# Attention beside a dense layer: where a short piece of beside-work stands between the scores and values of two steps

## The chip, the cores and the metric

The kernel runs on one core of a Trainium2 chip. The metric is device time in microseconds, from one launch to its end, as the median of several runs. Engines are named as the profile names them: PE is TensorE (PEld its weight loads), ACT is ScalarE, DVE is VectorE, POOL is GpSimd, SP the engine that issues transfers.

## What is computed

A block of a transformer on x of shape 2 x 2048 x 1024: attention with small latents, then a dense layer with eight LoRA updates folded in, both with a residual.

```python
def attention(x, ...):           # 32 heads, latents: q 12, k and v 4
    C_q = x @ Wq_d + bq_d
    C_kv = x @ Wkv_d + bkv_d
    q = (C_q @ W_qk + b_qk).reshape(b, s, 32, 4)
    scores = einsum('bqhd,bkd->bhqk', q, C_kv) / sqrt(4)
    attn = softmax(scores, axis=-1)
    V = (C_kv @ Wv_u + bv_u).reshape(b, s, 32, 32)
    out = einsum('bhqk,bkhd->bqhd', attn, V)
    return out.reshape(b, s, 1024) @ Wo + bo

x = x + attention(layernorm(x), ...)
x = x + layernorm(x) @ W.T + bias + lora(layernorm(x))
```

## The kernel before

**Stages.** The kernel has a first stage (statistics, latents and queries, up to 105.8 us in the trace), an attention stage (105.8 to 2017 us) and a tail for the last 512 rows (to 2077.6 us). The change lies in the attention stage only.

**Chunks and steps.** The 4096 rows are eight chunks of 512 queries. A chunk has 128 steps (`STEPS`): eight groups of four heads, and for each group 16 tiles of 128 keys. A step has three parts:

- `scores(step)` (L892 to L905): four products of 27 rows each on PE, one for each head, written to 4 of the 6 PSUM banks that hold scores (`SCORE_SLOTS` = 3 slots of two banks). It waits until the exponentials of an earlier step have read the banks that it overwrites: the wait is `exp_done` of the first exponential of the step before.
- two exponentials on ACT (L634), each 128 x 1024, from PSUM to `probs`, a ring of three steps. The first one of a step also waits until `values` of three steps before has read its slot of the ring.
- `values(step)` (L907 to L915): four products with 32 columns each on PE (two passes each in the trace, so 8 matmul records a step), from `probs` into the PSUM bank `SUMS`. They run two to three steps behind the scores.

**What runs beside.** PE works off, between those, the pieces of other work that `beside` names. One piece belongs to each odd step. For chunks 1 to 7 (`dense_beside`) they are the back half of the chunk before: turning the sums (`turn_o`, `turn_back`), the output projection (`project`, three products), turning the normed rows (`turn_y`, eight pieces a chunk of four transpositions each, L943), and the dense layer (`dense_burst`, 44 pieces a chunk of 4 or 5 products of 512 columns, L959). All of these write one PSUM bank, `SHARED`, and DVE empties it between them. For chunk 0 (`prepare`) they are the preparation of the dense weights. Its main part are sixteen pairs: `turn_w(k)` (four transpositions of the weights, L868) and, one pair of steps later, `lora_update(k)` (one product of 512 columns, two passes in the trace, L873). After each of the two DVE runs its part of `move_w(k)` (L1374 to L1383): a copy behind the transpositions, and behind the product an addition (L1381), a rounding copy (L1184) and a subtraction (L1186), both of the last two into `w_eff`. `turn_w(k)` waits in `free_bank` for the semaphore `prep_ok`, which the last of these, for k - 1, raises.

**What sets the order.** It is written out by hand in `attention`. PE runs its instructions in the order of the code and stands at each wait. In an even step `s` and the odd one behind it the order is: scores(s), values(s-2), values(s-1), scores(s+1), the piece beside step s+1. The other engines have programs of their own and are tied to PE by semaphores alone.

Of the kernel before, what the change touches and what calls it, by code (L numbers as in the profile page):

```python
# [33 lines left out]
def build_block(nc, x, wq_d, bq_d, w_qk, b_qk, wkv_d, bkv_d, wv_u, bv_u, wo, bo,  # L34
# [14 lines left out]
    CHUNKS = T // N  # L49
    CB = S // N  # L50
    TT = N // P
    KT = S // P
    KB = D // P
    G4 = H // 4
# [18 lines left out]
    with ExitStack() as ctx:  # L73
# [113 lines left out]
        prep_ok = sem("prep_ok")  # L187
# [29 lines left out]
        bound_read = sem("bound_read")  # L217
# [18 lines left out]
        q_loaded = [sem("q_loaded0"), sem("q_loaded1")]  # L236
# [3 lines left out]
        o_moved = sem("o_moved")  # L240
# [7 lines left out]
        ffn_moved = sem("ffn_moved")  # L248
# [19 lines left out]
        STEPS = G4 * KT  # L268
        BEHIND = 2
        UNITS = 2 * TT  # L270

        START = 2
# [3 lines left out]
        Q_LOADS = 16 * 4  # L276
# [5 lines left out]
        SCORE_SLOTS = 3  # L282
        SUMS, SHARED = 6, 7
# [5 lines left out]
        TURN_BACK_AT = BEHIND + 3  # L289
        FIRST_AT = BEHIND + 5  # L290
        TILE_AT, NEXT_AT, DENSE_AT = [], [], []
        at = FIRST_AT + 4
        for t in range(TT):
            if t == 2:
                TURN_AT = at
# [6 lines left out]
            at = low[-1] + 2  # L302
# [356 lines left out]
        def _(pe):  # L659
# [113 lines left out]
            def keep_busy(times, bank):  # L773
                for _ in range(times):
                    nc.tensor.transpose(ps[:, bank, 0:P], wqk_sb[:, :], ident[:, :])  # L775
# [100 lines left out]
            def prepare(g, kt):  # L876
                step = g * KT + kt
                if step == VALUES_AT:
                    turn_values()
                if step in (VALUES_AT + 2, VALUES_AT + 4):  # L880
                    turn_lora(PREP_LORA + (step - VALUES_AT) // 4)
                if WO_AT <= step < WO_AT + 16 and step % 2:
                    i = (step - WO_AT) // 2
                    times_wo(PREP_VO + i // 2, lv if i < 4 else bv_wide, i % 2)
                if step in (BIAS_AT, BIAS_AT + 2):
                    sum_bias(PREP_BIAS + (step - BIAS_AT) // 2)
                for k in range(2 * KB):
                    at = W_AT + 4 * k if k < W_BEFORE else TURN_0_AT + 2 + 4 * (k - W_BEFORE)
                    if step == at:
                        turn_w(k)  # L890
                    if step == at + 2:
                        lora_update(k)  # L892


            def scores(c, b, step, first):

                g, kt = divmod(step, KT)
                i = 2 * (c * STEPS + step)
                if step or not first:
                    pe.wait_ge(exp_done, i - 1)  # L900
                for h in range(4):
                    at = 2 * ((i + h // 2) % SCORE_SLOTS) + h % 2
                    last = nc.tensor.matmul(ps[:, at, :], key_t[TILE * h:TILE * h + KEYS, bass.ts(b * KT + kt, P)],  # L903
                                            q_in[TILE * h:TILE * h + KEYS, g % 2, :], start=True, stop=True)
                    if h % 2:  # L905
                        last.then_inc(s_ready, 1)

            def values(c, b, step):

                g, kt = divmod(step, KT)  # L910
                at = CW - W5 * (g % 4)
                pe.wait_ge(exp_done, 2 * (c * STEPS + step) + 2)
                for h in range(4):
                    last = nc.tensor.matmul(ps[32 * h:32 * h + 32, SUMS, :], c_wide[:, b * KT + kt, at:at + 32],  # L914
                                            probs[:, (c * STEPS + step) % PROBS, bass.ts(h, N)], start=(kt == 0 and g % 4 == 0),  # L915
                                            stop=(kt == KT - 1 and g % 4 == 3))
                last.then_inc(pv_done, 1)

            def turn_o(c, half):

                pe.wait_ge(o_moved, 2 * c + half + 1)
                for t in range(TT):
                    last = nc.tensor.transpose(ps[:, SHARED, bass.ts(t, P)], o_sb[:, bass.ts(t, P)], ident[:, :])
                last.then_inc(o_turned, 1)
# [39 lines left out]
            def dense_beside(c, step):  # L964

                p = c - 1
                if step == TURN_BACK_AT:
                    turn_back(p)
                if step == FIRST_AT:
                    pe.wait_ge(o_t_ready, p + 1)  # L970
                    project(p, 0, 0, SHARED)
                if step == FIRST_AT + 2:
                    pe.wait_ge(y_ready, START + p * TT * 2 + 1)
                    project(p, 0, 1, SHARED)
                if step == TURN_AT:
                    pe.wait_ge(ffn_moved, START + (p * TT + 2) * 2)
                    turn_o(c, 0)
                for t in range(TT):
                    if step == TILE_AT[t]:
                        if t == 2:  # L980
                            pe.wait_ge(o_normed, 2 * c + 1)
                        elif t:
                            pe.wait_ge(ffn_moved, START + (p * TT + t) * 2)
                        pe.wait_ge(y_ready, START + (p * TT + t + 1) * 2)
                        turn_y(p, t, 0, SHARED)
                    if step == TILE_AT[t] + 2:
                        pe.wait_ge(t_moved, START + CHUNKS * KB + (p * TT + t) * 2 + 1)
                        turn_y(p, t, 1, SHARED)
                    if t < TT - 1 and step == NEXT_AT[t]:
                        pe.wait_ge(ffn_moved, START + (p * TT + t) * 2 + 1)  # L990
                        project(p, t + 1, 0, SHARED)
                    if t < TT - 1 and step == NEXT_AT[t] + 2:
                        pe.wait_ge(y_ready, START + (p * TT + t + 1) * 2 + 1)
                        project(p, t + 1, 1, SHARED)
                    for half in range(2):
                        if step in DENSE_AT[t][half]:
                            j = DENSE_AT[t][half].index(step)
                            if j == 0 and half == 0:
                                pe.wait_ge(t_moved, START + CHUNKS * KB + (p * TT + t + 1) * 2)
                            elif j == 0 and t < TT - 1:  # L1000
                                pe.wait_ge(y_ready, START + (p * TT + t + 2) * 2)
                            elif j == 0:
                                pe.wait_ge(ffn_moved, START + (p * TT + t) * 2 + 1)
                            dense_burst(p, t, half, j)

            def attention(c, b, b_before=None):
                first = b_before is None
                for g in range(G4):
                    for kt in range(KT):
                        step = g * KT + kt  # L1010
                        scores(c, b, step, first)
                        if first and step < BEHIND:
                            keep_busy(8, SHARED if step else 2 * SCORE_SLOTS - 1)
                        if kt == KT - 1 and c * G4 + g + 1 < CHUNKS * G4:
                            pe.wait_ge(q_loaded[(g + 1) % 2], ((c * G4 + g + 1) // 2 + 1) * Q_LOADS)
                        if step % 2 == 0:
                            if step == 0 and not first:
                                values(c - 1, b_before, STEPS - 2)
                                values(c - 1, b_before, STEPS - 1)
                            if step:  # L1020
                                if first and step == BEHIND:
                                    pe.wait_ge(bound_read, 2)
                                if (step - BEHIND) % (4 * KT) == 0 and not (first and g == 0):
                                    pe.wait_ge(o_moved, 2 * c + g // 4)
                                values(c, b, step - 2)
                                values(c, b, step - 1)
                        if kt == BEHIND + 1 and g == 0 and not first:

                            pe.wait_ge(ffn_moved, START + (c - 1) * TT * 2)
                            turn_o(c - 1, 1)  # L1030
                        if first and step == TURN_0_AT:
                            pe.wait_ge(prep_ok, PREP_W + 2 * W_BEFORE)
                            turn_o(c, 0)
                        if first:
                            prepare(g, kt)
                        else:
                            dense_beside(c, step)

            pe.wait_ge(q_loaded[0], Q_LOADS)
            attention(0, 0)  # L1040
# [513 lines left out]
```

## Time and profile before

| | us |
|---|---|
| median of 3 runs | 2078.73 |
| lowest and highest run | 2078.69, 2080.83 |
| the profiled execution | 2079.62 |
| its span, first to last instruction | 2077.6 |
| up to the first exponential | 105.8 |
| chunk 0 of the attention (first exponential to that of chunk 1) | 237.50 |
| each of chunks 2 to 6 | 239.07 to 239.09 |
| from the last exponential's start | 61.6 |

PE is busy 94% of the span, ACT 95%, DVE 23%, POOL 10%. The busy time of an engine is the union of its instructions; exponentials overlap by about a tenth of a microsecond, so a late start of less than that does not show as idle time, and the start times have to be read. In what follows a pair of steps is called by the piece beside it, and the length of a pair is the time from one pair's first scores to the next one's.

### The profile page before, as it was taken

To read this page: it belongs to the slowest core of one execution; us is meant where nothing else is said; L and a number is where in the kernel's file an instruction comes from. 1 tells how busy PE (TensorE), PEld (TensorE's weight loads), DVE (VectorE), ACT (ScalarE), POOL (GpSimd) and SP (SyncE) were. 2 spreads that over 40 slices of the span, in tenths; PEclk is the share of its full clock that TensorE was granted. 3 is DMA by queue.
4 is the path that set the end of the run, shared out by engine and by line. 5 is a ranking of instruction groups with operands and counts; after the bars stand their busy time and mean duration, and the time that the engine had idled before them with its cause. 6 is when DMAs were issued, how large, how long until landed. Compare 5 with 4: busy or idle time off the path is not lost.

```text
span 2077.6 us, 36033 instructions
## 1 busy us (share of the span) xinstructions
PE 1962.2 (94%) x15085; PEld 715.1 (34%) x15085; DVE 475.6 (23%) x1140; ACT 1969.5 (95%) x2185; POOL 214.9 (10%) x220
## 2 busy tenths in 40 slices
PE   7979898999999999999999999999999999999999
PEld 4522222333333333333333333333333333333337
DVE  7713333111121211211121111212111111212115
ACT  5799999999999999999999999999999999999980
POOL 5600000000110002000110001100110001100022
PEclk9999999999999999999999999999999999999999
DMA  8442000000010001000010000100010000100011
GB/s 308 147 137 86 3 26 26 5 25 13 26 35 15 13 26 46 5 13 26 26 35 3 26 25 13 36 15 26 13 46 5 26 13 26 35 15 13 26 41 41
DMA packets 45806, 77.42 MB, mean 37 GB/s; under 512 B 15886, under 2 KB 29766, under 8 KB 45642
## 3 DMA queue, kind: packets, MB, share of 16 engines
q1 hardware_dynamic: 43296, 75.02, 10.7%
q8 instruction: 119, 1.95, 0.4%
q10 hardware_dynamic: 2346, 0.09, 0.1%
q14 instruction: 45, 0.37, 0.1%
HBM read 51.23 MB, written 23.86 MB: 36 GB/s over the span
## 4 chain that ended last, share of the span: by engine, by line
ACT 43%; PE 35%; issue 16%; DVE 0%; DVEq 0%
ACT probs L634 43%; PE ps L914 17%; PE ps L959 10%; PE ps L903 6%; PE ps L948 2%; PE ps L937 0%; PE ps L943 0%; PE ps L775 0%; DVE y L1433 0%; PE ps L1056 0%; PE ps L1052 0%; DVE o_t L1489 0%; ACT o_t L649 0%; ACT o_sb L646 0%; DVE recip L1481 0%
## 5 line engine op out<-in xcount | busy, mean ns | idle before, releaser
L634 ACT ACTIVATE probs<-ps 128x1024 f32<-128x1024 f32 x2048 | 1899.8, 1030 | 17.7 <-PE ps L903 7.1
L914 PE MATMUL ps<-probs,c_wide 128*32 128x512 f32 x8192 | 985.7, 599 | 0.0
L903 PE MATMUL ps<-q_in,key_t 27*128 27x512 bf16 x4096 | 404.2, 385 | 94.1 <-ACT probs L634 90.8
L959 PE MATMUL ps<-w_eff,xn_t 128*128 128x512 f32 x1344 | 394.5, 418 | 0.0
L914 PEld LDWEIGHTS ps<-probs,c_wide 128*32 128x32 f32 x8192 | 212.3, 108 | 424.9 <-issue 220.0
L903 PEld LDWEIGHTS ps<-q_in,key_t 27*128 27x128 bf16 x4096 | 103.0, 91 | 722.7 <-ACT probs L634 715.2
L1433 DVE SCALAR_TENSOR_TENSOR y<-ps,nw,y 128x512 f32<-128x512 f32 x64 | 48.1, 751 | 979.0 <-PE ps L959 967.6
L959 PEld LDWEIGHTS ps<-w_eff,xn_t 128*128 128x128 f32 x1344 | 228.2, 188 | 102.1 <-issue 69.8
L536 POOL TENSOR_TENSOR y<-y,ffn_bias 128x1024 f32<-128x1024 f32 x32 | 76.4, 2388 | 1349.9 <-DVEq L1454 1349.9
L531 POOL TENSOR_TENSOR y<-y,attn_bias 128x1024 f32<-128x1024 f32 x32 | 75.9, 2385 | 463.9 <-DMA y<-in_L_attn_x_dram 463.8
L1417 DVE TENSOR_TENSOR y<-ps,y 128x512 f32<-128x512 f32 x56 | 38.7, 692 | 134.9 <-PE ps L937 134.9
L1184 DVE CAST xn_t<-ps 128x512 fp32r<-128x512 f32 x56 | 38.8, 692 | 123.3 <-PE ps L943 123.3
L937 PE MATMUL ps<-w_vo,o_t 128*128 128x512 f32 x192 | 60.4, 426 | 0.3 <-DVE o_t L1489 0.3
L556 ACT ACTIVATE area<-ps 128x512 f32<-128x512 f32 x64 | 35.3, 616 | 26.4 <-PE ps L678 22.0
L948 PE MATMUL ps<-w_eff,xn_t 128*128 128x512 f32 x192 | 44.7, 391 | 0.0
L943 PE MATMUL ps<-ident,y 128*128 128x128 f32 x256 | 41.0, 285 | 0.1
L1186 DVE TENSOR_TENSOR xn_t<-ps,xn_t 128x512 fp32r<-128x512 f32 x56 | 38.8, 692 | 9.8 <-DVEq L1120 9.8
L1420 DVE BATCH_NORM_STATS2 stats<-y 128x6 f32<-128x512 f32 x56 | 38.9, 695 | 1.9
L948 PEld LDWEIGHTS ps<-w_eff,xn_t 128*128 128x128 f32 x192 | 35.8, 188 | 7.3
L937 PEld LDWEIGHTS ps<-w_vo,o_t 128*128 128x128 f32 x192 | 31.4, 188 | 16.4 <-issue 12.7
L654 ACT ACTIVATE xn_t<-ps 128x512 fp32r<-128x512 f32 x8 | 4.4, 596 | 34.1 <-PE ps L943 34.1
L943 PEld LDWEIGHTS ps<-ident,y 128*128 128x128 f32 x256 | 27.1, 140 | 13.7 <-issue 13.3
(168 smaller groups left out, 619.7 us busy)
## 6 DMA issues: line engine op xcount, KB each, us to landing
y<-in_L_attn_x_dram SPq DMA_DIRECT2D x40, 512.0 KB, 4.3
out_dram<-y SPq DMA_DIRECT2D x31, 512.0 KB, 2.7
area<-in_L_attn_x_dram SPq DMA_DIRECT2D x16, 512.0 KB, 9.1
q_in<-q_parts SPq DMA_DIRECT2D x256, 27.0 KB
q_parts<-q_parts_sb SPq DMA_DIRECT2D x48, 128.0 KB, 2.8
xn<-in_L_attn_x_dram SPq DMA_DIRECT2D x8, 512.0 KB, 7.7
y<-in_L_attn_Wo_dram SPq DMA_DIRECT2D x1, 2048.0 KB, 8.6
xn<-in_L_attn_Wo_dram SPq DMA_DIRECT2D x1, 2048.0 KB, 13.3
```

What stands on the lines that cost most here:

```text
L531: pool.tensor_tensor(y[:, t, :], y[:, t, :], attn_bias[:, :], ALU.add).then_inc(xb_ready, 1)
L536: pool.tensor_tensor(y[:, t, :], y[:, t, :], ffn_bias[:, :], ALU.add).then_inc(yb_ready, 1)
L634: nc.scalar.activation(probs[:, (c * STEPS + step) % PROBS, bass.ts(pair, 2 * N)], ps[:, 2 * (i % SCORE_SLOTS):2 * (i % SCORE_SLOTS) + 2, ...
L903: last = nc.tensor.matmul(ps[:, at, :], key_t[TILE * h:TILE * h + KEYS, bass.ts(b * KT + kt, P)], q_in[TILE * h:TILE * h + KEYS, g % 2, :] ...
L914: last = nc.tensor.matmul(ps[32 * h:32 * h + 32, SUMS, :], c_wide[:, b * KT + kt, at:at + 32], probs[:, (c * STEPS + step) % PROBS, bass.t ...
L937: last = nc.tensor.matmul(ps[:, bank, :], o_t[:, a, bass.ts(t, P)], w_vo[:, b, bass.ts(n, N)], start=(i == 0), stop=(i == 2))
L943: last = nc.tensor.transpose(ps[:, bank, bass.ts(a, P)], y[:, t, bass.ts(4 * u + a, P)], ident[:, :])
L948: last = nc.tensor.matmul(ps[:, bank, :], xn_t[:, t % 2, a, kb, :], w_eff[:, b, kb, bass.ts(half, N)], start=(kb + i == 0), stop=(kb == KB ...
L959: last = nc.tensor.matmul(ps[:, SHARED, :], xn_t[:, t % 2, a, kb, :], w_eff[:, b, kb, bass.ts(half, N)], start=(kb + i == 0), stop=(kb == ...
L1184: ch.then(nc.vector.tensor_copy(high, bank_part))
L1420: ch.put(nc.vector.bn_stats(stats[:, t, n, :], y[:, t, bass.ts(n, N)]))
L1433: nc.vector.scalar_tensor_tensor(out=y[:, t, bass.ts(half, N)], in0=ps[:, bank, :], scalar=nw[:, 0, 3, t:t + 1], in1=y[:, t, bass.ts(half, ...
```

## The change

In the pairs whose piece is a set of transpositions, and in pairs of chunk 0 that have no piece left, the piece and the scores of the second step go between the two sets of values. All other pairs keep their order. The loop body is split into two helpers, `score` (the scores with their waits) and `beside` (the piece with its waits).

```diff
+            TURN_STEPS = [BEHIND + 1, TURN_BACK_AT, TURN_AT] + [at + 2 * u for at in TILE_AT for u in range(2)]
+            PREP_TURN_STEPS = [W_AT + 4 * k if k < W_BEFORE else TURN_0_AT + 2 + 4 * (k - W_BEFORE) for k in range(2 * KB)]
+            PREP_LAST = PREP_TURN_STEPS[-1] + 2
...
+                for step in range(0, STEPS, 2):
+                    score(step)
+                    if first:
+                        between = step and (step + 1 in PREP_TURN_STEPS or step + 1 > PREP_LAST)
+                    else:
+                        between = step + 1 in TURN_STEPS
+                    if step:
...
+                        values(c, b, step - 2)
+                    elif not first:
+                        values(c - 1, b_before, STEPS - 2)
+                        values(c - 1, b_before, STEPS - 1)
+                    if between:
+                        beside(step + 1)
+                        score(step + 1)
+                        values(c, b, step - 1)
+                    else:
+                        if step:
+                            values(c, b, step - 1)
+                        score(step + 1)
+                        beside(step + 1)
```

With the numbers of this kernel, `TURN_STEPS` are the odd steps 3, 5, 11, 13, 41, 43, 71, 73, 75, 103 and 105: eleven pairs in each of chunks 1 to 7, in five groups of neighbours (2, 2, 2, 3 and 2). `PREP_TURN_STEPS` are 53, 57, 69, 73 and so on by fours to 121: sixteen pairs of chunk 0, each with a `lora_update` pair behind it. Behind them steps 125 and 127 have no piece. Only PE's order changes; ACT, DVE, POOL and SP run the same instructions in the same order.

PE in chunk 0, around one `turn_w` (L868) between two `lora_update` (L873). `ps` is the PSUM, L903 are scores, L914 values (four products a step), `xn` holds the weights to be turned here. Before:

```order
L903 MATMUL ps<-q_in,key_t 128x512 x4
L873 MATMUL ps<-lora_bt,lora_a_sb 128x512
L903 MATMUL ps<-q_in,key_t 128x512 x4
L914 MATMUL ps<-probs,c_wide 32x512 x8
L903 MATMUL ps<-q_in,key_t 128x512 x4
L868 MATMUL ps<-ident,xn 128x128 x4
L903 MATMUL ps<-q_in,key_t 128x512 x4
L914 MATMUL ps<-probs,c_wide 32x512 x8
L903 MATMUL ps<-q_in,key_t 128x512 x4
L873 MATMUL ps<-lora_bt,lora_a_sb 128x512
```

And now:

```order
L903 MATMUL ps<-q_in,key_t 128x512 x4
L873 MATMUL ps<-lora_bt,lora_a_sb 128x512
L903 MATMUL ps<-q_in,key_t 128x512 x4
L914 MATMUL ps<-probs,c_wide 32x512 x4
L868 MATMUL ps<-ident,xn 128x128 x4
L903 MATMUL ps<-q_in,key_t 128x512 x4
L914 MATMUL ps<-probs,c_wide 32x512 x4
L903 MATMUL ps<-q_in,key_t 128x512 x4
L914 MATMUL ps<-probs,c_wide 32x512 x8
L903 MATMUL ps<-q_in,key_t 128x512 x4
L873 MATMUL ps<-lora_bt,lora_a_sb 128x512
```

The transpositions stand one set of values and one set of scores nearer to the product before them.

PE in a chunk from 1 on, at two neighbouring `turn_y` pairs (L943, which turns rows of `y`) behind a projection (L937). Before:

```order
L937 MATMUL ps<-w_vo,o_t 128x512 x3
L903 MATMUL ps<-q_in,key_t 128x512 x4
L914 MATMUL ps<-probs,c_wide 32x512 x8
L903 MATMUL ps<-q_in,key_t 128x512 x4
L943 MATMUL ps<-ident,y 128x128 x4
L903 MATMUL ps<-q_in,key_t 128x512 x4
L914 MATMUL ps<-probs,c_wide 32x512 x8
L903 MATMUL ps<-q_in,key_t 128x512 x4
L943 MATMUL ps<-ident,y 128x128 x4
```

And now:

```order
L937 MATMUL ps<-w_vo,o_t 128x512 x3
L903 MATMUL ps<-q_in,key_t 128x512 x4
L914 MATMUL ps<-probs,c_wide 32x512 x4
L943 MATMUL ps<-ident,y 128x128 x4
L903 MATMUL ps<-q_in,key_t 128x512 x4
L914 MATMUL ps<-probs,c_wide 32x512 x4
L903 MATMUL ps<-q_in,key_t 128x512 x4
L914 MATMUL ps<-probs,c_wide 32x512 x4
L943 MATMUL ps<-ident,y 128x128 x4
L903 MATMUL ps<-q_in,key_t 128x512 x4
L914 MATMUL ps<-probs,c_wide 32x512 x4
```

The second scores of such a pair no longer stand behind the values of step s-1.

## Rows read from the trace of the kernel before

**Rows 1.** The page's costliest group: line, operation, count | busy us, mean ns | idle.

```profile
L634 ACT ACTIVATE probs<-ps 128x1024 f32<-128x1024 f32 x2048 | 1899.8, 1030 | 17.7 <-PE ps L903 7.1
```

**Rows 2.** Table by stretch, chunks 0 and 3: length, busy time by engine, clock.

```profile
core 0: us, PE busy (x) PEld busy (x) DVE busy (x) ACT busy (x) POOL busy (x), PEclk, DMA share, GB/s
105.78:343.28 237.50, 205.47 (x1725) 56.63 (x1728) 72.40 (x123) 236.56 (x257) 9.50 (x4) 0.99 0.19 60
821.50:1060.57 239.07, 230.38 (x1800) 80.50 (x1796) 41.34 (x107) 237.57 (x257) 18.95 (x8) 1.00 0.07 22
```

**Rows 3.** Timeline of PE, one pair of chunk 1: start us, length, what.

```profile
502.76 0.40 PE L903 MATMUL ps<-q_in,key_t 27*128 27x512 bf16 x4
503.08 1.92 PE L914 MATMUL ps<-probs,c_wide 128*32 128x512 f32 x16
504.94 0.39 PE L903 MATMUL ps<-q_in,key_t 27*128 27x512 bf16 x4
505.27 1.20 PE L959 MATMUL ps<-w_eff,xn_t 128*128 128x512 f32 x4
506.45 0.40 PE L903 MATMUL ps<-q_in,key_t 27*128 27x512 bf16 x4
```

**Rows 4.** Timeline of ACT there, single exponentials (507.19 left out).

```profile
504.40 1.04 ACT L634 ACTIVATE probs<-ps 128x1024 f32<-128x1024 f32 x1
505.37 1.03 ACT L634 ACTIVATE probs<-ps 128x1024 f32<-128x1024 f32 x1
506.29 1.02 ACT L634 ACTIVATE probs<-ps 128x1024 f32<-128x1024 f32 x1
...
508.10 1.04 ACT L634 ACTIVATE probs<-ps 128x1024 f32<-128x1024 f32 x1
```

**Rows 5.** Timeline of ACT, neighbouring exponentials at the attention's start.

```profile
106.70 1.02 ACT L634 ACTIVATE probs<-ps 128x1024 f32<-128x1024 f32 x1
107.60 1.03 ACT L634 ACTIVATE probs<-ps 128x1024 f32<-128x1024 f32 x1
```

**Rows 6.** Chain of waits, pairs with five products beside: start, us, what.

```profile
518.10 1.85 PE ps L914 x16
519.95 0.33 PE ps L903 x4
520.28 1.36 PE ps L959 x5
521.63 0.33 PE ps L903 x4
```

**Rows 7.** Timeline of chunk 0, one cycle from `lora_update` to `lora_update`.

```profile
297.07 1.12 PE L873 MATMUL ps<-lora_bt,lora_a_sb 128*128 128x512 f32 x2
298.25 0.40 PE L903 MATMUL ps<-q_in,key_t 27*128 27x512 bf16 x4
...
299.78 0.69 DVE L1186 TENSOR_TENSOR w_eff<-part_f,w_eff 128x512 fp32r<-128x512 f32 x1 [0.18 <-DVEq L1120]
300.44 0.40 PE L903 MATMUL ps<-q_in,key_t 27*128 27x512 bf16 x4
300.76 0.66 PE L868 MATMUL ps<-ident,xn 128*128 128x128 f32 x4
...
304.45 1.13 PE L873 MATMUL ps<-lora_bt,lora_a_sb 128*128 128x512 f32 x2
```

**Rows 8.** Timeline of chunk 0, the one `turn_w` that waited for DVE.

```profile
322.40 0.69 DVE L1186 TENSOR_TENSOR w_eff<-part_f,w_eff 128x512 fp32r<-128x512 f32 x1 [0.18 <-DVEq L1120]
323.15 0.66 PE L868 MATMUL ps<-ident,xn 128*128 128x128 f32 x4 [0.18 <-DVE w_eff L1186]
```

**Rows 9.** Timeline of PE, first stage, transpositions with work right behind them.

```profile
50.17 0.66 PE L678 MATMUL ps<-ident,area 128*128 128x128 f32 x4
50.67 0.60 PE L722 MATMUL ps<-ident,lat 128*128 128x128 f32 x4
```

**Rows 10.** Timeline of chunk 3, the first `turn_y` pair behind a dense half.

```profile
895.41 0.75 DVE L1433 SCALAR_TENSOR_TENSOR y<-ps,nw,y 128x512 f32<-128x512 f32 x1 [18.04 <-PE ps L959]
897.79 0.66 PE L943 MATMUL ps<-ident,y 128*128 128x128 f32 x4
898.97 0.39 PE L903 MATMUL ps<-q_in,key_t 27*128 27x512 bf16 x4 [0.53 <-ACT probs L634]
```

**Rows 11.** Table by stretch, 3.4 us at the attention's start.

```profile
107.30:110.70 3.40, 3.40 (x20) 1.83 (x24) 1.55 (x3) 3.34 (x5) 0.00 (x0) 0.51 0.63 63
```

More of the change, by code:

```diff
@@ L1004, in dense_beside @@
                             dense_burst(p, t, half, j)
+            TURN_STEPS = [BEHIND + 1, TURN_BACK_AT, TURN_AT] + [at + 2 * u for at in TILE_AT for u in range(2)]
+            PREP_TURN_STEPS = [W_AT + 4 * k if k < W_BEFORE else TURN_0_AT + 2 + 4 * (k - W_BEFORE) for k in range(2 * KB)]
+            PREP_LAST = PREP_TURN_STEPS[-1] + 2
             def attention(c, b, b_before=None):
                 first = b_before is None
[L1008 to L1037, printed above, removed]
@@ new lines, in score, with beside @@
+                def score(step):
+                    scores(c, b, step, first)
+                    g, kt = divmod(step, KT)
+                    if first and step < BEHIND:
+                        keep_busy(8, SHARED if step else 2 * SCORE_SLOTS - 1)
+                    if kt == KT - 1 and c * G4 + g + 1 < CHUNKS * G4:
+                        pe.wait_ge(q_loaded[(g + 1) % 2], ((c * G4 + g + 1) // 2 + 1) * Q_LOADS)
+                def beside(step):
+                    if step == BEHIND + 1 and not first:
+                        pe.wait_ge(ffn_moved, START + (c - 1) * TT * 2)
+                        turn_o(c - 1, 1)
+                    if first and step == TURN_0_AT:
+                        pe.wait_ge(prep_ok, PREP_W + 2 * W_BEFORE)
+                        turn_o(c, 0)
+                    if first:
+                        prepare(*divmod(step, KT))
+                    else:
+                        dense_beside(c, step)
@@ new lines, in attention @@
+                for step in range(0, STEPS, 2):
+                    score(step)
+                    if first:
+                        between = step and (step + 1 in PREP_TURN_STEPS or step + 1 > PREP_LAST)
+                    else:
+                        between = step + 1 in TURN_STEPS
+                    if step:
+                        if first and step == BEHIND:
+                            pe.wait_ge(bound_read, 2)
+                        if (step - BEHIND) % (4 * KT) == 0 and not (first and step == BEHIND):
+                            pe.wait_ge(o_moved, 2 * c + step // (4 * KT))
+                        values(c, b, step - 2)
[6 more added lines that the diff above has]
+                        values(c, b, step - 1)
+                    else:
+                        if step:
+                            values(c, b, step - 1)
+                        score(step + 1)
+                        beside(step + 1)
```

## The prediction, made before the changed kernel was run

> **What bounds the kernel now.** I began with the page's costliest groups: 2048 exponentials on ACT, 1899.8 us busy and 17.7 us idle [rows 1]. The table by stretch says the same of each chunk: ACT is busy 236.56 of 237.50 us in chunk 0 and 237.57 of 239.07 in chunk 3, beside a PE that is busy 205 and 230 us [rows 2]. That looks like a full ACT, and the start times show that it is not quite one. Two exponentials that wait for nothing start 0.90 us apart (106.70, 107.60) [rows 5], and from 506.29 to 508.10 there are two such distances, 0.905 each [rows 4]. So four exponentials, a pair of steps, could take 3.61 us. The pair in the timeline takes 3.69: from scores at 502.76 to scores at 506.45 [rows 3].
>
> The timelines show what the 0.08 us are. The distances between exponentials are 0.97 (504.40 to 505.37), 0.92 (to 506.29), 0.90 and 0.90 [rows 4]. The late one is the first exponential of the second step, and it is late by PE's order: its scores stand behind both sets of values. Read as a ring it is: exponential, 1.03 long, and 0.05 until PE starts the first scores; 0.32 until the values; 1.86 for both sets of values (503.08 to 504.94); 0.43 until the exponential of the second scores (504.94 to 505.37) [rows 3, 4]. The sum, 1.08 + 0.32 + 1.86 + 0.43 = 3.69, is the length of the pair. The piece beside is not in that ring as long as it ends before 1.08 + 0.43 = 1.51 us after the second scores began. With five products it does not: 0.33 + 1.85 + 0.33 + 1.36 = 3.87 us, and PE alone sets the pair [rows 6]. The change does not touch those pairs. So each pair is bound by one of three: ACT at 3.61, the ring at 3.69, PE at 3.87.
>
> **The pairs of chunks 1 to 7.** In a moved pair the second scores come behind one set of values and the transpositions. I price these: half of 1.86 is 0.93, and I allow 1.00, since leaving 32-column products costs once more. For four transpositions the rows bound the time until something else can start: 0.50 (50.17 to 50.67, other transpositions behind) [rows 9] and 0.66, their whole busy time [rows 10]. I take 0.58, between the two, as scores are products of another shape but the busy time overlaps what follows by 0.07, as in 0.40 against 0.32 for scores [rows 3]. The way from the first exponential to that of the next moved scores is then 1.08 + 0.32 + 1.00 + 0.58 + 0.43 = 3.41 us (3.49 with 0.66), under ACT's 3.61. The other conditions hold too: scores(s+1) need the first exponential of step s, 1.51 us against a distance of 1.81; values(s-1) end 1.3 us after scores(s+1) start, while scores(s+2) may start after 1.51 and the slot of the ring of three is wanted later. So ACT sets a moved pair.
>
> The transpositions start 1.18 us earlier in the pair than now. In the tightest place, a tile's first `turn_y`, DVE's addition ends at 895.41 + 0.75 = 896.16 and the transpositions now start at 897.79, so that 896.61 is still 0.45 late enough [rows 10]. The other turns read what DVE finished a pair before, or stand behind a turn that has itself moved; I cost them at nothing. If the cover were gone, PE would stand and the 3.41 would grow, up to 0.2 us of it free.
>
> The gain: an exponential behind a late one comes at 0.92, so the first moved pair of a group gives 3.69 - (0.92 + 3 x 0.903) = 0.06 us, a later one 3.69 - 3.61 = 0.08. The pair behind a group is back in the ring at 3.69. A chunk has five groups with eleven pairs: 5 x 0.061 + 6 x 0.078 = 0.77 us, and seven chunks **gain 5.4 us**. Bounds: nothing, if ACT has a slower floor than the two rows show; and no more than this, as ACT can't go below it.
>
> **The pairs of chunk 0.** Here the moved transpositions have a wait that is now covered. `turn_w(k)` needs the whole of `move_w(k-1)` on DVE, which starts behind `lora_update(k-1)`. In the rows the product starts at 297.07 and DVE's subtraction ends at 299.78 + 0.69 = 300.47, 3.40 later. Now the transpositions stand behind the second scores of the next pair, at 300.76, so that DVE is just done [rows 7]. In the new order they could go at 298.25 + 0.32 + 1.00 = 299.57 and have to stand until 300.47 plus the way from DVE to PE. That way is 0.06 us: once in this trace `turn_w` did wait, and started at 323.15 behind an end at 323.09 [rows 8]. PE stands 0.96 us at the wait, and behind it in its queue are scores(s+1), the values and the scores of the next pair; ACT waits for the first of those. No other engine is late by it.
>
> The cycle from one `lora_update` to the next, step by step: 3.40 to the end on DVE, 0.06 to PE, 0.58 for the transpositions, 0.43 from the scores to the exponential, 1.08 from the exponential to the first scores of the unmoved pair behind, 0.33, 1.86 for both sets of values, 0.32 for the second scores. Sum 8.06 us, against 304.45 - 297.07 = 7.38 now [rows 7]: 0.68 more. It happens for k = 1 and for k = 3 to 15, 14 times: 9.5 us. `turn_w(0)` and `turn_w(2)` have no `lora_update` in the pair before them, so these two gain 0.06 each, and the two pairs without a piece at the end gain 0.06 + 0.08. The chunk's boundary may give back 0.1. Chunk 0 **loses 9.2 to 9.3 us**. Bounds of the stall term: with 0.50 for the transpositions 14 x 0.60 = 8.4, with 0.66 14 x 0.76 = 10.6.
>
> **Sum.** 9.2 - 5.4 = +3.8 us, on the profiled execution 2079.62 + 3.8 = 2083.4. That execution was 0.9 above the median of the runs, so the median goes from 2078.73 to **2082.5 us**, 0.18% more. The bounds of the terms give 2081.4 to 2083.6. A measurement here can tell about 0.2% (4.2 us, 2082.9) from no change, so my likeliest case ends just inside that.
>
> **Rivals.**
>
> *The stall is covered, and the kernel gets faster.* If DVE's `move_w` were done by the time PE arrives at the moved transpositions, all sixteen `turn_w` pairs would gain 0.06 and chunk 0 would give 16 x 0.06 + 0.14 + 0.1 = 1.2 us on top of 5.4: 2072.1 us. It decides at 299.57 against 300.53 in the rows; DVE would have to be a full microsecond quicker from the product's start, with three dependent operations in between. For it speaks only that DVE has nothing else to do there. 5%.
>
> *ACT does not close up.* If the moved pairs stay at 3.69 for a reason of ACT's own, only the loss is left: 2078.73 + 9.5 = 2088.2 us. For it: no pair of this trace runs at 3.61 from end to end. Against it: two distances of 0.90 in a row behind a late one [rows 4] and one of two first steps [rows 5]. The Trainium skill (ScalarE: Activation LUTs, What ACT_TABLE_LOAD costs) gives 186 ns plus 0.833 ns an element for an ACTIVATE with immediates and an overlap of 93 ns, for 1024 elements an estimate of 0.95 us from start to start; by that rule four take 3.78 and nothing at all could be gained. The pair of 3.69 is already below it. 7%.
>
> *PE's clock falls in chunk 0.* At the start of the attention, where PE had stood idle and then did transpositions only, the granted clock was 0.51, the lower of the levels 1.2 and 2.4 GHz, for 3.4 us [rows 11]. If the new stalls brought that on, each fall would cost at most 1.7 us (3.4 us at half speed do 1.7 us of work), from 2084.2 for one to 2106 for one in each of the 14 cycles. Against it: PE stays busy for some 6.8 of the 8.06 us of the stalled cycle (four scores at 0.32, two times 1.86, 0.58 and 1.12), and the clock is 1.00 in the chunks [rows 2]. The Trainium skill (TensorE: Matmul & The Clock Gate, Part 4: PE-mode transpose) says that transpositions do not count as PE activity in the way of products; by that rule the moved stretch, stall and transpositions together, is the likeliest place for a fall. 4%.
>
> *It is as reckoned*, with the loss of chunk 0 larger than the gain of the others. 84%.
>
> **How the numbers follow.** The likeliest case is 2082.5, with 2081.2 to 2083.9 as its own range. Leaving out 2 in 10, I take 2080.6 to 2084.6, which has room for a half-covered stall, for one fall of the clock and for the run-to-run spread of the runs shown (2078.69 to 2080.83). Slower by over 0.2%, above 2082.9: four tenths of the likeliest case, 0.33, with 0.07 and 0.03 of the rivals, 0.43. Faster: 0.05. Within: 0.52.
>
> **What would show it.** The table by stretch: chunk 0 near 246.8 us instead of 237.50, each of chunks 2 to 6 near 238.3 instead of 239.07. The waits: PE at L868 on DVE `w_eff` for 0.9 to 1.0 us, 14 times. Exponentials 0.90 apart through a moved pair of a later chunk. A chunk 0 of 236 us would make the stall wrong, later chunks of 239.1 the gain, and a clock under 0.98 in chunk 0 the assumption that it holds.

## The result

The changed kernel takes 2086.64 us (median of 8 runs, 2084.94 to 2088.84) against 2079.68 us for the kernel before (8 runs, 2078.69 to 2080.83). The ratio is 1.0034, with a 95% interval of 1.0025 to 1.0044: 7.0 us **slower**. The forecast was 3.8 us slower, 2082.5 us, with a range from 2080.6 to 2084.6 us. The profiled execution took 2088.10 us, its span is 2086.3 us.

Shown are the page's costliest group, then the table by stretch: chunk 0, chunk 1, chunk 3 and what follows the last exponential's start (columns: length, busy time by engine, clock, DMA).

```profile
L634 ACT ACTIVATE probs<-ps 128x1024 f32<-128x1024 f32 x2048 | 1898.9, 1041 | 26.2 <-PE ps L903 15.7
```

```profile
core 0: us, PE busy (x) PEld busy (x) DVE busy (x) ACT busy (x) POOL busy (x), PEclk, DMA share, GB/s
105.67:352.61 246.94, 208.84 (x1725) 54.93 (x1728) 72.07 (x123) 237.51 (x256) 9.48 (x4) 0.99 0.18 58
352.61:591.59 238.98, 232.06 (x1800) 79.38 (x1796) 41.21 (x106) 237.48 (x258) 14.26 (x6) 1.00 0.05 15
830.38:1069.18 238.80, 231.88 (x1800) 79.39 (x1796) 41.34 (x107) 237.31 (x258) 18.99 (x8) 1.00 0.07 22
2023.48:2086.30 62.82, 58.28 (x273) 46.17 (x272) 32.64 (x97) 7.20 (x18) 14.41 (x6) 0.97 0.17 59
```

Beside [rows 2]: chunk 0 went from 237.50 to 246.94, 9.4 us more and as forecast (246.8); 0.14 of it lie in the last but one of the stalls below, where DVE's rounding copy took 0.57 us in this execution and 0.43 elsewhere. Chunk 3 went from 239.07 to 238.80. It should have been 238.3, so a chunk gained 0.27 us and not 0.77. That is where the forecast fails. The tail is 1.2 us longer in this one execution, with a clock of 0.97; more on that below. In the group row the mean exponential is 1041 ns where it was 1030 [rows 1]: exponentials in the moved pairs are recorded as longer, and the rows of ACT below show how.

**The stall in chunk 0**, in the waits of PE alone and in the timeline of one cycle (start us, length, engine, what):

```profile
PE ps L868 <- DVE w_eff L1205: 12.5, 14, 1.0
```

```profile
303.02 1.12 PE L873 MATMUL ps<-lora_bt,lora_a_sb 128*128 128x512 f32 x2
304.20 0.40 PE L903 MATMUL ps<-q_in,key_t 27*128 27x512 bf16 x4
304.53 1.07 PE L914 MATMUL ps<-probs,c_wide 128*32 128x512 f32 x8
...
305.72 0.69 DVE L1205 TENSOR_TENSOR w_eff<-part_f,w_eff 128x512 fp32r<-128x512 f32 x1 [0.18 <-DVEq L1139]
306.47 0.66 PE L868 MATMUL ps<-ident,xn 128*128 128x128 f32 x4 [0.88 <-DVE w_eff L1205]
307.06 0.39 PE L903 MATMUL ps<-q_in,key_t 27*128 27x512 bf16 x4
```

It stands 14 times. From the product's start at 303.02 to DVE's end at 306.41 are 3.39 us (forecast 3.40), 0.06 to PE, 0.59 until the scores (forecast 0.58). Beside [rows 7] the transpositions no longer find DVE done.

**The moved pairs of a later chunk.** The timeline of ACT in chunk 3, single exponentials of the two `turn_y` pairs (steps 10 to 13) and the first late one behind them; several between them are left out:

```profile
848.79 1.03 ACT L634 ACTIVATE probs<-ps 128x1024 f32<-128x1024 f32 x1
850.60 1.05 ACT L634 ACTIVATE probs<-ps 128x1024 f32<-128x1024 f32 x1
852.41 1.08 ACT L634 ACTIVATE probs<-ps 128x1024 f32<-128x1024 f32 x1
854.21 1.10 ACT L634 ACTIVATE probs<-ps 128x1024 f32<-128x1024 f32 x1
856.93 1.14 ACT L634 ACTIVATE probs<-ps 128x1024 f32<-128x1024 f32 x1
857.99 1.03 ACT L634 ACTIVATE probs<-ps 128x1024 f32<-128x1024 f32 x1
```

The first and the fifth row lie nine exponentials apart: (856.93 - 848.79) / 9 = 0.904 us from start to start, as forecast. But the durations climb from 1.03 to 1.14, 12.5 ns with each exponential. The ends are 849.82 and 858.07, so **an exponential is finished every 0.917 us**, not every 0.904. PE waits for ends, as its scores show (timeline of PE, the pair behind the group):

```profile
855.37 0.39 PE L903 MATMUL ps<-q_in,key_t 27*128 27x512 bf16 x4 [0.37 <-ACT probs L634]
855.70 1.92 PE L914 MATMUL ps<-probs,c_wide 128*32 128x512 f32 x16
857.55 0.40 PE L903 MATMUL ps<-q_in,key_t 27*128 27x512 bf16 x4
```

The scores at 855.37 wait for the exponential that started at 854.21 and ended at 855.32, and from there the ring runs as ever: 0.32, 1.86 and 0.43 to the exponential at 857.99. It starts 1.06 us behind the one before instead of 0.97 [rows 4]. What the starts had won in the group is given back there, except for some 0.024 us a pair: 3.690 - 4 x 0.917 = 0.022, and by the chunks (239.07 - 238.80) / 11 = 0.025.

### The profile page after: what moved, and what is told of

Read it like the earlier page. It is cut to its first block, busy times and chain, and to the rows that moved or that the text cites. A ratio compares the mean times of both kernels' runs of the same rounds, so it can differ in the third digit from the quotient of the medians.

```text
span 2086.3 us, 36034 instructions
## 1 busy us (share of the span) xinstructions
PE 1977.5 (95%) x15085; PEld 706.9 (34%) x15085; DVE 475.3 (23%) x1140; ACT 1968.8 (94%) x2185; POOL 215.3 (10%) x220
## 4 chain that ended last, share of the span: by engine, by line
ACT 38%; PE 35%; issue 11%; DVE 0%; DVEq 0%
ACT probs L634 38%; PE ps L914 16%; PE ps L959 10%; PE ps L903 6%; PE ps L948 2%; PE ps L937 0%; PE ps L943 0%; PE ps L1075 0%; DVE y L1452 0%; DVE w_eff L1205 0%; PE ps L868 0%; PE ps L1071 0%; DVE o_t L1508 0%; ACT o_t L649 0%; ACT o_sb L646 0%
## 5 line engine op out<-in xcount | busy, mean ns | idle before, releaser
L634 ACT ACTIVATE probs<-ps 128x1024 f32<-128x1024 f32 x2048 | 1898.9, 1041 | 26.2 <-PE ps L903 15.7
L914 PE MATMUL ps<-probs,c_wide 128*32 128x512 f32 x8192 | 1005.3, 600 | 0.0
L903 PE MATMUL ps<-q_in,key_t 27*128 27x512 bf16 x4096 | 404.1, 385 | 75.4 <-ACT probs L634 70.3
L903 PEld LDWEIGHTS ps<-q_in,key_t 27*128 27x128 bf16 x4096 | 102.9, 91 | 705.8 <-ACT probs L634 697.8
L914 PEld LDWEIGHTS ps<-probs,c_wide 128*32 128x32 f32 x8192 | 202.9, 108 | 389.2 <-issue 224.7
L937 PE MATMUL ps<-w_vo,o_t 128*128 128x512 f32 x192 | 61.9, 435 | 0.3 <-DVE o_t L1508 0.3
L943 PEld LDWEIGHTS ps<-ident,y 128*128 128x128 f32 x256 | 27.2, 140 | 47.5 <-issue 29.3
L943 PE MATMUL ps<-ident,y 128*128 128x128 f32 x256 | 40.9, 285 | 0.0
L937 PEld LDWEIGHTS ps<-w_vo,o_t 128*128 128x128 f32 x192 | 32.4, 193 | 16.6 <-issue 12.7
```

Source lines behind the costliest of these rows:

```text
L634: nc.scalar.activation(probs[:, (c * STEPS + step) % PROBS, bass.ts(pair, 2 * N)], ps[:, 2 * (i % SCORE_SLOTS):2 * (i % SCORE_SLOTS) + 2, ...
L937: last = nc.tensor.matmul(ps[:, bank, :], o_t[:, a, bass.ts(t, P)], w_vo[:, b, bass.ts(n, N)], start=(i == 0), stop=(i == 2))
L943: last = nc.tensor.transpose(ps[:, bank, bass.ts(a, P)], y[:, t, bass.ts(4 * u + a, P)], ident[:, :])
```

## The experiments

All times are medians, each beside the median of the kernel before on the same chip; times of stretches are from the one trace of each version. A traced execution can lie some us off the median. "Theory of ends" is the reading above; "theory of starts" that of the prediction.

### Each half of the change alone

Chunk 0's `turn_w` pairs unmoved:

```diff
-                        between = step and (step + 1 in PREP_TURN_STEPS or step + 1 > PREP_LAST)
+                        between = step + 1 > PREP_LAST
```

> The changed kernel with the sixteen turn_w pairs of chunk 0 in their old order; the eleven pairs of each later chunk and the two pieceless pairs stay moved. Theory of ends: back to back, exponentials start 0.904 us apart but finish 0.917 apart, and the ring of the next unmoved pair starts from an end, so a moved pair gains 3.690 - 4 x 0.917 = 0.024 us and the 79 moved pairs 1.9 us in all; with the boundary of chunk 0, 2.0 us faster than before. Theory of starts (the one of the prediction): 5.6 us faster. Either way chunk 0 is back at 237.4 us and no turn_w waits for DVE. The chunks from 2 on: 238.80 us by ends, 238.30 by starts.

Measured: 2077.36 us against 2079.34, ratio 0.9991 (0.9982 to 1.0000), 2.0 us faster. Table by stretch, chunks 0 and 3:

```profile
105.71:343.72 238.01, 206.50 (x1725) 57.21 (x1729) 72.14 (x123) 236.51 (x256) 9.49 (x4) 0.99 0.19 60
821.48:1060.26 238.78, 231.88 (x1800) 79.41 (x1796) 41.34 (x107) 237.29 (x258) 18.95 (x8) 1.00 0.07 22
```

The gain is the 2.0 of the theory of ends, and the 5.6 of the theory of starts are outside the interval (up to 3.7). Chunk 3 is at 238.78 (238.80 by ends, 238.30 by starts). Chunk 0 is 0.6 longer than expected, because the clock was at half for 6.8 us around its start where it was for 3.4 in the first trace of the kernel before: its first two pairs take 9.11 us against 8.44 there.

Chunk 0's `turn_w` pairs alone:

```diff
-                        between = step and (step + 1 in PREP_TURN_STEPS or step + 1 > PREP_LAST)
+                        between = step and step + 1 in PREP_TURN_STEPS
                     else:
-                        between = step + 1 in TURN_STEPS
+                        between = False
```

> Only the sixteen turn_w pairs of chunk 0 are moved, everything else is in the old order. If the loss is the 14 stalls of PE behind DVE's subtraction, chunk 0 takes 246.9 us, 9.5 more, later chunks 239.07, and the whole is 9.5 us slower than before. A rival, by which part of the loss belongs to the later chunks or the tail, has chunk 0 longer by less and the whole slower by clearly under 9 us.

Measured: 2089.02 us against 2079.34, ratio 1.0046 (1.0032 to 1.0059), 9.7 us slower. Chunk 3 is at 239.05 us again, chunk 0 at 246.24:

```profile
106.22:352.46 246.24, 207.15 (x1725) 54.55 (x1728) 72.21 (x123) 237.56 (x256) 9.48 (x4) 1.00 0.19 58
830.69:1069.74 239.05, 230.34 (x1800) 80.47 (x1796) 41.34 (x107) 237.56 (x257) 18.98 (x8) 1.00 0.07 22
```

This execution had no half clock at the start, which makes chunk 0 shorter by 1.0 us (last experiment). Against that, its last stall but one was 0.28 us longer than the others, as DVE's rounding copy took 0.71 us there. With both set right chunk 0 is at 247.0, against the 246.9 expected. The rival, by which part of the loss lies in the later chunks or the tail, is out. The halves add up: 9.7 - 2.0 = 7.7, beside 7.0 measured for both.

### What the transpositions wait for

The change as it is, with DVE releasing the bank as soon as it has read it:

```diff
                 ch.then(nc.vector.tensor_tensor(base, ps[:, SHARED, :], base, ALU.add))
                 ch.end()
-                split_three_pass(w_eff[:, 0, kb, cols], w_eff[:, 1, kb, cols], base, prep_ok)
+                dve.sem_inc(prep_ok, 1)
+                split_three_pass(w_eff[:, 0, kb, cols], w_eff[:, 1, kb, cols], base, w_split)
...
             pe.wait_ge(prep_ok, PREP_ALL)
+            pe.wait_ge(w_split, 2 * KB)
```

> The changed kernel as it is, but DVE gives the shared bank free right behind the addition that reads it (L1381 of before) and not behind the two operations on w_eff that follow; those raise a semaphore of their own, which PE awaits before chunk 1. DVE's way from the product's start to the release falls from 3.40 to some 2.1 us, under the 2.5 us that PE takes to the transpositions. If that wait is the loss of chunk 0, it falls to 237.1 us and the whole is 2.4 us faster than before (6.5 by the theory of starts). If anything else about the place of the transpositions is the loss, chunk 0 stays near 247.

Measured: 2077.23 us against 2079.34, ratio 0.9990 (0.9981 to 0.9999), 2.1 us faster. Timeline of chunk 0 (line numbers are one higher on PE; L869 are the transpositions):

```profile
297.19 1.12 PE L874 MATMUL ps<-lora_bt,lora_a_sb 128*128 128x512 f32 x2
298.37 0.39 PE L904 MATMUL ps<-q_in,key_t 27*128 27x512 bf16 x4
298.42 0.69 DVE L1402 TENSOR_TENSOR part_f<-ps,part_f 128x512 f32<-128x512 f32 x1 [4.50 <-PE ps L874]
...
299.69 0.66 PE L869 MATMUL ps<-ident,xn 128*128 128x128 f32 x4
299.99 0.69 DVE L1207 TENSOR_TENSOR w_eff<-part_f,w_eff 128x512 fp32r<-128x512 f32 x1 [0.18 <-DVEq L1141]
```

The transpositions start 1.32 us behind the scores, where the forecast put them (1.32 for scores and one set of values), with no idle time of PE, and before DVE's subtraction begins. Chunk 0 takes 236.95 us where the change took 246.94. Both executions had 3.4 us of half clock at the start. So the loss of chunk 0 is the wait for all of `move_w`, and of that the part that only concerns `w_eff`. The rest is the theory of ends once more: 2.1 us gained where 2.4 were due by ends and 6.5 by starts.

### The piece behind the second values

The moved pairs in the order scores, values, scores, values, piece:

```diff
                     if between:
-                        beside(step + 1)
                         score(step + 1)
                         values(c, b, step - 1)
+                        beside(step + 1)
```

> The same pairs as in the change, in the order scores, values, scores, values, piece: the scores of the second step are freed from the second values, but the transpositions stay at the end of the pair. They then start 2.64 us into the pair (two scores at 0.32 and two values at 1.00), behind DVE's end at 2.22 into it, so the stall should be gone: chunk 0 at 237.1 us. By ends the whole is 2.4 us faster than before (95 moved pairs of 0.024 and the boundary), by starts 6.5 us faster. A rival, by which it is the freed scores themselves that cost chunk 0 its 9.5 us, leaves chunk 0 near 247.

Measured: 2082.14 us against 2079.34, ratio 1.0013 (1.0004 to 1.0022), 2.8 us slower. A miss of both theories. Table by stretch, chunks 0 and 3, and the timeline of PE at the end of the same two `turn_y` pairs:

```profile
104.85:342.00 237.15, 206.46 (x1725) 54.30 (x1728) 72.21 (x123) 237.12 (x256) 9.48 (x4) 1.00 0.20 60
820.52:1059.68 239.16, 231.86 (x1800) 79.38 (x1796) 41.33 (x107) 237.66 (x257) 18.98 (x8) 1.00 0.07 22
```

```profile
843.75 0.39 PE L903 MATMUL ps<-q_in,key_t 27*128 27x512 bf16 x4 [0.37 <-ACT probs L634]
844.07 1.06 PE L914 MATMUL ps<-probs,c_wide 128*32 128x512 f32 x8
845.07 0.66 PE L943 MATMUL ps<-ident,y 128*128 128x128 f32 x4
845.66 0.39 PE L903 MATMUL ps<-q_in,key_t 27*128 27x512 bf16 x4
845.98 1.92 PE L914 MATMUL ps<-probs,c_wide 128*32 128x512 f32 x16
```

The stall is gone here too: chunk 0 is at 237.15, not 247 (with the full clock at its start, worth 1.0), so it is not the freed scores that cost 9.5 us. But a chunk now takes 239.16, more than the 239.07 of the kernel before. The trace is of the fastest of the eleven runs (2078.91), with the clock full throughout; it is 0.5 us above the median (2078.4) of the eight runs of the kernel before that had the full clock too. The remaining 2.3 us of the 2.8 lie in executions with falls of the clock, of which this version has no trace. The scores that open the pair behind the group start at 845.66 with no wait for ACT before them: PE comes to them late, with values and transpositions (0.32 + 1.00 + 0.59 = 1.91 us) behind scores that had themselves waited for an exponential. ACT has a reserve against that inside the group; the ring behind it has none. That PE's lateness is the whole of the 0.37 us between this chunk and that of the change is worked out from these rows and not tested by itself. In chunk 0 the pairs alternate, each moved one has an unmoved one behind it, and the same cost falls due sixteen times: by the first exponentials of the pairs, a moved pair takes 3.61 us and the one behind it 3.82, together 0.05 more than two unmoved ones, where the version with the early release has 3.62 and 3.74, 0.03 less.

### ACT's floor, with nothing beside

The early release, and the pairs of chunk 0 without a piece moved as well:

```diff
+            IDLE_STEPS = [s for s in range(5, TURN_0_AT, 2) if s < VALUES_AT or BIAS_AT + 2 < s < W_AT or s > W_AT + 4 * W_BEFORE - 2]
...
-                        between = step and (step + 1 in PREP_TURN_STEPS or step + 1 > PREP_LAST)
+                        between = step and (step + 1 in PREP_TURN_STEPS or step + 1 > PREP_LAST or step + 1 in IDLE_STEPS)
```

> The early release of the bank with 14 pairs more of chunk 0 moved, those that have no piece beside them: steps 4 to 18 (eight pairs in a row, 32 exponentials), 46 to 50 and 60 to 64. It measures ACT's floor with nothing beside on PE. Theory of ends: in the row of eight the starts stay 0.904 apart, each exponential lasts 12.5 ns longer than the one before, to 1.03 + 32 x 0.0125 = 1.43 us, and the pair behind the row pays all of it, its second scores' exponential coming some 0.40 us later than in a pair of the ring, 1.36 instead of 0.96 behind the one before; or the starts fall to 0.917 apart once the two are too far from each other. Either way a moved pair gains 0.024 us, chunk 0 goes from 236.9 to 236.6 and the whole is 2.4 us faster than before. A rival, that it is the transpositions beside that lengthen the exponentials: then these pairs show durations that stay near 1.03, the row of eight gains 0.078 a pair, and chunk 0 falls to 235.9.

Measured: 2076.37 us against 2080.36, ratio 0.9984 (0.9975 to 0.9993), 4.0 us faster by the medians, 1.5 to 5.2 by the interval. The 2.4 expected lie within it, and the times do not tell this version from the one before; its trace does. Timeline of ACT in the row of eight pairs (single exponentials, those between left out) and the first one behind it, with one set of scores of PE in the same stretch:

```profile
116.49 1.09 ACT L635 ACTIVATE probs<-ps 128x1024 f32<-128x1024 f32 x1
123.72 1.19 ACT L635 ACTIVATE probs<-ps 128x1024 f32<-128x1024 f32 x1
131.86 1.30 ACT L635 ACTIVATE probs<-ps 128x1024 f32<-128x1024 f32 x1
135.49 1.35 ACT L635 ACTIVATE probs<-ps 128x1024 f32<-128x1024 f32 x1
136.41 1.34 ACT L635 ACTIVATE probs<-ps 128x1024 f32<-128x1024 f32 x1
136.89 0.39 PE L904 MATMUL ps<-q_in,key_t 27*128 27x512 bf16 x4 [0.44 <-ACT probs L635]
137.32 1.35 ACT L635 ACTIVATE probs<-ps 128x1024 f32<-128x1024 f32 x1
...
143.16 1.02 ACT L635 ACTIVATE probs<-ps 128x1024 f32<-128x1024 f32 x1
```

From 116.49 to 131.86 are 17 exponentials: starts 0.904 apart, ends (117.58 and 133.16) 0.917 apart. The duration climbs by 12.5 ns each, with no piece on PE, so transpositions have nothing to do with it, and the rival is out. PE's scores come early enough there: the exponential at 131.86 starts 0.47 us behind its scores, where one that waits for them starts 0.43 behind. So nothing but ACT holds the ends at 0.917, and that is ACT's floor for this instruction. It settles the question of the two theories.

At 1.35 us the climb stops, and the starts themselves fall to 0.91 to 0.92 apart (136.41, 137.32). What stops it is the ring between ACT and PE, and not a limit of ACT that these rows could show: the scores at 136.89 wait for the exponential that started at 135.49 and ended at 136.83, and the exponential of these scores starts at 137.32, 0.43 behind them. Two exponentials then take 1.35 + 0.06 + 0.43 = 1.83 us, 2 x 0.917, and the starts can run ahead no further. This is read from the rows and not tested by an edit; how long durations could grow with more banks for scores is open. The exponential behind the row is the one at 143.16, a late one with its 1.02 us; the pair in which it stands takes 4.01 us where its like take 3.69, which pays back what the starts had won.

Chunk 0 is at 235.37 us, 1.6 less than in the version before it. Of that 1.0 is the clock at its start, full in this execution; 0.34 are the 14 pairs; and the three pairs at steps 16, 48 and 64 had been 0.09 longer than their neighbours in every trace with the old order, which they are no longer. The reason of that is open. So what the theory of ends says of the 14 pairs is met; the rest by which chunk 0 lies under the 236.6 expected is the clock and these three pairs.

### The clock in the first pairs and in the tail

Four single executions, of the two kernels unchanged.

> The kernel before, unchanged, for a second trace. Its first trace has one stretch of 3.4 us with the granted clock at half, at the start of the attention. Theory of the clock: these stretches come and go between executions of the same program, at the start of the attention (1.0 us each, from the first pairs of steps there) and in the tail (1.5 us each), and the eight chunks in between keep their times to 0.1 us. Then the time is 2078.6, 2079.6 or 2081.1 us for none, the first, or both. A rival, that the spread lies in the chunks themselves, has chunks that differ between the traces by more than that.

> The kernel before once more, for a third trace, with the same expectations: 2078.6, 2079.6 or 2081.1 us by the falls of the clock, and chunks equal to 0.1 us.

> The changed kernel, unchanged, for a second trace. Its first trace has two stretches of half clock, one at the start of the attention and one in the tail, and took 2088.1 us, 1.5 more than the median of its runs. Theory of the clock: without the second it takes 2086.6 us, without both 2085.6, with chunk 0 at 246.9 (246.0 without the fall at its start) and the later ones at 238.80 in every trace. A rival, that the change lengthens the tail by itself, has the tail 1.2 us longer than that of the kernel before also with no fall in it.

> The changed kernel once more, for a third trace, with the same expectations: 2085.6, 2086.6 or 2088.1 us by the falls of the clock, and chunks from 2 on at 238.80 us.

Measured: 2079.16 and 2079.57 us for the kernel before, 2087.07 and 2086.30 for the changed one. Table by stretch: the changed kernel's second of these (chunk 0, chunk 3, tail), then 6.8 us at the start of the attention in the first one of the kernel before, then 3.4 us in the tail of the changed kernel's first trace:

```profile
106.27:352.09 245.82, 207.44 (x1725) 54.31 (x1728) 71.93 (x123) 237.41 (x257) 9.48 (x4) 1.00 0.19 58
830.10:1068.90 238.80, 231.89 (x1800) 79.43 (x1800) 41.34 (x106) 237.29 (x257) 18.99 (x8) 1.00 0.07 22
2022.88:2084.50 61.62, 57.02 (x273) 44.96 (x272) 32.62 (x97) 7.22 (x18) 14.42 (x6) 1.00 0.17 60
```

```profile
103.30:110.10 6.80, 5.96 (x32) 3.67 (x36) 2.31 (x5) 4.31 (x5) 0.00 (x0) 0.50 0.52 70
```

```profile
2028.80:2032.20 3.40, 3.40 (x11) 2.62 (x10) 1.41 (x6) 0.49 (x2) 2.38 (x1) 0.50 0.45 146
```

The granted clock at the start of the attention was full in this trace; it was at 0.50 for 3.4 us in the changed kernel's other two traces, and for 3.4, 6.8 and 3.4 us in those of the kernel before. Chunk 0 is 245.82 us with it full and 246.94 in the changed kernel's first trace: 0.99 of the 1.12 us lie in the first two pairs, where the clock fell, and 0.14 in the one long stall. Where the 3.4 us began before the first exponential (the second trace of the changed kernel and the third of the kernel before), the first two pairs lost 0.6 to 0.7 us, and with 6.8 us 1.7. The tail is 61.62 us with the clock full and 62.82 with the fall. Chunk 3 is the same to 0.02 us. So the change does not lengthen the tail: the rival is out. The times by the sum of falls were only half met. For no fall 2086.30 was measured where 2085.6 was expected; 0.6 of the 0.7 us lie in the first stage, as the first exponential started at 106.27 and not at 105.67. Over all traces of this study that start lies between 104.53 and 106.33, and no run here shows why.

## Why the prediction was wrong

**Right: what binds a pair.** The three bounds (ACT, the ring over both sets of values, PE) were the right ones for the pairs of the kernel before and of the change, with ACT's own put too low. The ring of 3.69 from four terms stood in all traces. Not explained are three pairs of chunk 0, at steps 16, 48 and 64, with 3.78.

**Right: the price of chunk 0.** A cycle of 8.06 us was forecast; `lora_update` starts at 303.02 and the next at 311.07, 8.05. Fourteen stalls of 0.9 to 1.0 us, as said. Chunk 0 is 9.4 us longer, 9.3 without what is peculiar to one stall, with 3.4 us of half clock at its start in both traces; the forecast had 9.2 to 9.3. The early release and the unmoved pairs both show that the stall, and its wait, is the whole of it. The faster rival, a covered stall, was wrong as it stood, but its mechanism is what the early release makes true.

**Wrong: the size of one term, the gain of a moved pair.** The step that failed is "ACT sets a moved pair" at 3.61 us, four times the 0.90 between two starts. That distance was read correctly and holds, but it is not the rate at which ACT finishes. The floor is 4 x 0.917 = 3.67, so a pair gains 0.024 us and not 0.06 to 0.08: 7 x 0.27 = 1.9 us in all instead of 5.4. The upper bound that I gave for this term, "as ACT can't go below it", was the right kind of sentence with the wrong number, and the lower bound, nothing, was nearer. That lower bound was written down and then left out of the sum: the "bounds of the terms" of 2081.4 to 2083.6 vary the stall alone, and with no gain they would have reached past 2087. The rival of an ACT that does not close up had the direction and 7%: it was two thirds true. The numbers were in the rows: the exponentials at 506.29 and 508.10 in [rows 4], two apart, last 1.02 and 1.04 us, and [rows 5] shows 1.02 and 1.03 for two neighbours. I read the first column and not the second.

With 1.9 in the place of 5.4 the sum is 9.2 - 1.9 = +7.3 us, against 7.0 measured. That the two agree to 0.3 us is within the noise of such a difference. The median of the kernel before moved up as well, from 2078.73 in three runs to 2079.68 in eight, and accounts for 0.95 of the 4.1 us between the forecast and the time; the other 3.2 are the 3.5 by which the gain was too large, within the noise.

**The clock** did fall, but not in the stalls: chunk 0 shows 0.99 in one trace and 1.00 in another, with the same 14 stalls. It fell at the start of the attention, as in the kernel before, and once in the tail, where no trace of the kernel before has it but that of the early release has. The prediction made the stretch of [rows 11] one of transpositions only; the timeline has scores and values in it as well. The working time of PE in a stalled cycle, given as 6.8 us, adds up to 6.7. That transpositions do not count as PE activity in the way of products, as the Trainium skill has it (TensorE: Matmul & The Clock Gate, Part 4), was not seen to act there. The other rule of the Trainium skill (ScalarE: Activation LUTs, What ACT_TABLE_LOAD costs) gave 0.95 us an exponential; the runs have 0.917, below it and above my 0.904. Its consequence, no gain at all, was nearer to the 1.9 us than my 5.4.

## What to carry to other kernels

Read an engine's floor from the ends of its instructions, start plus duration, over ten or more in a row: starts can run ahead of ends for a long while, and only ends release anybody. Before moving a piece of work forward in an engine's order, ask for each of its waits when it is met, and whether the waiter needs all that the semaphore stands for; here the release stood two operations behind the last read of the bank, and raising it there turned 7 us lost into 2 us gained. And a gap that is closed in the starts of one pair comes back in the next pair that is bound by a ring; only the difference of the two rates stays.

## What the runs showed of the hardware

- Back-to-back exponentials of 128 x 1024 on ACT start 0.904 us apart and end 0.917 apart. Their recorded duration grows by 12.5 ns each, from 1.03 to 1.35 us over 26 of them in the row of eight moved pairs, where, by the rows, the ring with PE stops it. The first one behind a wait for its scores lasts 1.02 again.
- The granted clock of TensorE falls to half (0.50, the lower of the levels 1.2 and 2.4 GHz) for 3.4 us, in some executions and not in others of the same program: around the start of the attention (twice for 6.8 us), where PE had been idle for 1.4 us in the executions with a fall and without; in the tail; and in two traces at 37.5 us in the first stage. A fall of 3.4 us costs 0.6 to 1.0 us at the start of the attention and 1.1 to 1.2 in the tail. Stalls of 0.95 us in every 8.06 did not bring it on.
